# Four expert blocks per round on TensorE, their transpositions in one row, gathers two blocks and stores six blocks off the gate-up

## What is computed

```python
def step(out, ws):
    wg, wu, wd, we = ws
    inter = jax.nn.silu(x @ wg.T) * (x @ wu.T)
    return (out + inter @ wd.T * we[:, None], None)
out, _ = jax.lax.scan(step, jnp.zeros_like(x), (gate_proj, up_proj, down_proj, w_full.T))
```

## Time and profile before

| | us |
|---|---|
| median of 3 runs | 1127.13 |
| lowest and highest run | 1126.86, 1133.95 |
| profiled execution, its own time | 1126.25 |
| span in its trace, first to last instruction | 1124.4 |
| expert stage, first gate-up to the last scaled row | 646.1 to 1078.2 |
| sum-up and output after it | 1078.2 to 1124.4 |

### The profile page before, as it was taken

How to read it: one execution, slowest core, us unless ns; L and a number is a source line. 1 busy time by engine, 2 the same in 40 slices (tenths; PEclk the granted TensorE clock), 3 DMA queues, 4 the chain that set the end, 5 groups by cost and what they waited for, 6 DMA issues and landing times. The chain is left out here.

```text
span 1124.4 us, 25144 instructions
## 1 busy us (share of the span) xinstructions
PE 1069.0 (95%) x7622; PEld 658.7 (59%) x7622; DVE 700.2 (62%) x2440; ACT 656.4 (58%) x1339; POOL 451.1 (40%) x521
## 2 busy tenths in 40 slices
PE   6889999999999999999889699999999999999997
PEld 3465666666666656664666445555555555555576
DVE  6866566665656666662459765656556666565648
ACT  4325454545555444547445668777877777787730
POOL 4333132222122000000220157777777777777620
PEclk9999999999999999999999899999999999999999
DMA  7501030113111311102113386583748546667278
GB/s 246 116 11 33 18 67 3 40 24 54 32 33 32 49 28 23 24 2 58 39 44 98 99 185 212 186 251 116 228 134 262 177 144 200 185 216 265 92 298 291
DMA packets 81789, 129.66 MB, mean 115 GB/s; under 512 B 32884, under 2 KB 53109, under 8 KB 81142
## 3 DMA queue, kind: packets, MB, share of 16 engines
q1 hardware_dynamic: 61852, 77.13, 24.7%
q0 software_dynamic: 15360, 47.21, 13.1%
q10 hardware_dynamic: 4448, 3.72, 1.1%
HBM read 97.57 MB, written 30.05 MB: 113 GB/s over the span
## 5 line engine op out<-in xcount | busy, mean ns | idle before, releaser
L710 DVE CUSTOM_DVE_ANT_0 a_masked<-a_ps_s,a_mask 128x512 bf16<-128x512 f32 (+3 forms) x512 | 230.3, 487 | 159.8 <-PE a_ps_s L877 157.6
L623 ACT ACTIVATE a_probs<-a_ps_e 128x512 f32<-128x512 f32 (+1 forms) x384 | 188.1, 527 | 119.7 <-PE a_ps_e L898 118.4
L1924 PE MATMUL e_ps_gu<-e_w_gu,e_xT 128*64 x640 | 208.7, 469 | 2.4 <-ACT e_s_gu L1737 1.6
L1924 PE MATMUL e_ps_gu<-e_s_gu,e_xT 128*64 128x352 f32 x640 | 208.6, 469 | 0.0
L188 POOL DMA_INDIRECT yn<-rows,inv x160 | 159.3, 995 | 118.9 <-DVE inv L1456 59.7
L1698 POOL DMA_INDIRECT y<-e_y,dst x160 | 163.8, 1024 | 59.0 <-issue 29.2
L1949 PE MATMUL e_ps_y<-e_w_d,e_hT 88*64 x640 | 151.5, 379 | 0.9 <-DVE e_hT L1814 0.9
L1949 PE MATMUL e_ps_y<-e_s_d,e_hT 88*64 88x256 f32 x640 | 151.5, 379 | 0.0
L895 PE MATMUL a_ps_e<-a_qT,a_kT 75*128 75x512 bf16 (+3 forms) x512 | 140.9, 303 | 2.1 <-ACT a_probs L623 1.6
L877 PE MATMUL a_ps_s<-a_kT,a_qT 72*128 72x512 bf16 (+3 forms) x512 | 131.4, 299 | 4.7 <-DVE a_headmax L710 2.8
L1924 PEld LDWEIGHTS e_ps_gu<-e_w_gu,e_xT 128*64 128x64 f32 x640 | 81.7, 137 | 92.0 <-issue 89.3
(11 more groups left out here) (259 smaller groups left out, 1873.5 us busy)
## 6 DMA issues: line engine op xcount, KB each, us to landing
e_w_gu<-e_gu SPq DMA_DIRECT2D x64, 352.0 KB
e_w_d<-e_down SPq DMA_DIRECT2D x64, 176.0 KB
a_qT<-qk_parts SPq DMA_DIRECT2D x45, 192.0 KB
e_w_gu<-y SPq DMA_DIRECT2D x8, 768.0 KB
qk_parts<-a_stage SPq DMA_DIRECT2D x16, 256.0 KB, 2.6
qkv<-y SPq DMA_DIRECT2D x12, 256.0 KB
e_w_d<-y SPq DMA_DIRECT2D x4, 768.0 KB
yn<-rows,inv POOLq DMA_INDIRECT x160, 3.3
```

The lines of the kernel that those rows point to most:

```text
L623: nc.scalar.activation(probs[:, i % HKV, UCOL[u]:UCOL[u + 1]], ps_e[:, (i * 3 + u) % 2, 0:w], ACT.Exp, scale=SCALE0).then_inc(exp_done, 1)
L710: ins = V.tensor_tensor_reduce(masked[:, n % 2, c:c + w], ps_s[:, n % 2, c:c + w], mask[:, T - w:T], 1.0, -3e38, ALU.add, ALU.max, headmax ...
L1924: ins = nc.tensor.matmul(ps_gu[r * SEG:(r + 1) * SEG, j % 2, 0:2 * INTER1], xT[:, j // 2 % 2, j % 2, k * P + r * SEG:k * P + (r + 1) * SEG ...
```

## The change

PE, ACT and DVE now go through groups of four blocks. On PE a group is: gate-up of two blocks, down of two blocks of the group before, gate-up of two, down of two, then all sixteen transpositions: `h` of the group's first two blocks, the rows of the next four blocks, `h` of the last two. Gate-up writes three PSUM banks in turn (the third is `ps_yT`), the turned rows two (`ps_o` is the second). Silu writes straight into `h`, which has four slots, and `gate` works in place. On DVE the copies follow the order of the row. POOL gathers `i + 8` and stores `i - 6` in step `i`.

```diff
-        LEAD, BEHIND, NF = 2, 4, ring.FIRST
+        LEAD, BEHIND, NF = 0, 6, ring.FIRST
...
+        gu_bank = (ps_gu[:, 0, :], ps_gu[:, 1, :], ps_yT[:, :])
+        xT_bank = (ps_xT[:, :], ps_o[:, :])
...
-                if j >= 2:
-                    act.wait_ge(h_ready, j - 1)
-                nc.scalar.activation(sg[:, j % 2, :], ps_gu[:, j % 2, 0:INTER1], ACT.Silu)\
+                if j >= 4:
+                    act.wait_ge(hT_ready, j - 3)
+                nc.scalar.activation(h[:, j % 4, :], gu_bank[j % 3][:, 0:INTER1], ACT.Silu)\
...
+            for g in range(FOURS):
+                j = 4 * g
+                for k in range(3):
+                    gate(j + k)
+                    attention(*part(j + k))
+                    if j == 0 and k == 1:
+                        copy_x(1)
+                        weigh(2)
+                        weigh(3)
+                gate(j + 3)
+                copy_h(2 * g)
+                if g + 1 < FOURS:
+                    copy_x(2 * g + 2)
+                    copy_x(2 * g + 3)
+                copy_h(2 * g + 1)
+                attention(*part(j + 3))
+                if g + 1 < FOURS:
+                    for k in range(4, 8):
+                        weigh(j + k)
...
-                if j >= 2 and j % 2 == 0:
-                    pe.wait_ge(xT_copied, j // 2)
+                if j >= 4 and j % 2 == 0:
+                    pe.wait_ge(xT_copied, j // 2 - 1)
...
                 pe.wait_ge(w_copied, gate_up_copied(j))
+                if j >= 3:
+                    pe.wait_ge(h_ready, j - 2)
...
-            oldest, now = None, [expert_of(j) for j in range(2)]
+            oldest, now = None, [expert_of(j) for j in range(4)]
+            for g in range(FOURS + 1):
                 after = None
+                b, a = 4 * g, 4 * g - 4
+                for k in (0, 2):
+                    if g < FOURS:
+                        gate_up(b + k, now[k])
+                        gate_up(b + k + 1, now[k + 1])
+                        if b + k == 0:
+                            turn_pair(1)
+                    if g:
+                        down(a + k, oldest[k])
+                        down(a + k + 1, oldest[k + 1])
+                if g + 1 < FOURS:
+                    after = [expert_of(b + 4 + k) for k in range(4)]
+                if g < FOURS:
+                    turn_h(2 * g)
+                    if g + 1 < FOURS:
+                        turn_pair(2 * g + 2)
+                        turn_pair(2 * g + 3)
+                    turn_h(2 * g + 1)
                 oldest, now = now, after
```

More of the change, by code:

```diff
@@ L1530, in layer1_experts @@
         NS, NW, NY, NQ = ring.NS, ring.NW, SCATTERS, 8
-        PAIRED = NBLK // 2
-        LEAD, BEHIND, NF = 2, 4, ring.FIRST
+        PAIRED, FOURS = NBLK // 2, NBLK // 4
+        LEAD, BEHIND, NF = 0, 6, ring.FIRST
         FIRST_ROWS_AT = 100
@@ L1539, in layer1_experts @@
         weight = sbuf(ctx, nc, "e_weight", [P, NQ])
-        sg = sbuf(ctx, nc, "e_sg", [P, 2, INTER1])
-        h = sbuf(ctx, nc, "e_h", [P, 2, INTER1])
+        h = sbuf(ctx, nc, "e_h", [P, 4, INTER1])
         hT = sbuf(ctx, nc, "e_hT", [HI1, 2, 2, 2 * P])
@@ L1613, in add_up @@
             E.tensor_tensor(x_sb[:, i, :], x_sb[:, i, :], y8[f][:, 0:D], ALU.add).then_inc(done, 1)
[L1615 to L1620, removed]
+        gu_bank = (ps_gu[:, 0, :], ps_gu[:, 1, :], ps_yT[:, :])
+        xT_bank = (ps_xT[:, :], ps_o[:, :])
         def gate_up_copied(j):
-            return j + 1 if j < 2 else 4 * (j // 2) - 2 + j % 2 + 1
+            g, k = divmod(j, 4)
+            if j < 4:
+                return j + 1
+            return 8 * g + k - 1 if k >= 2 else 8 * g + k - 3
         def down_copied(j):
-            return 4 * (j // 2) + j % 2 + (5 if j + 2 < NBLK else 3)
+            g, k = divmod(j, 4)
+            last_four = 0 if g < FOURS - 1 else 2 if k < 2 else 4
+            return 8 * g + (7 if k < 2 else 9) + k - last_four
         def part(j):
@@ L1748, in _, with silu_exp @@
                 copy_gate_up(j, experts[j])
[L1749 to L1760, removed]
+            def silu_exp(j):
+                silu(j)
+                n, l, k = part(j)
+                if k == 5:
+                    act.wait_ge(s_ready, n * B + B)
+                    nc.scalar.activation(e1[:, :, :], s1[:, :, :], ACT.Exp,
+                                         scale=SCALE1).then_inc(e_ready, 1)
+            for g in range(FOURS + 1):
+                b, a = 4 * g, 4 * g - 4
+                if g < FOURS:
+                    experts += [expert_of(b + 2), expert_of(b + 3)]
+                    for j in (b, b + 1):
+                        silu_exp(j)
+                        copy_gate_up(j + 2, experts[j + 2])
+                if g:
+                    for j in (a, a + 1):
+                        copy_y(j)
+                        copy_down(j + 2, experts[j + 2])
+                if g < FOURS:
+                    if g < FOURS - 1:
+                        experts += [expert_of(b + 4), expert_of(b + 5)]
+                    for j in (b + 2, b + 3):
+                        silu_exp(j)
                         if j + 2 < NBLK:
                             copy_gate_up(j + 2, experts[j + 2])
[L1763 to L1768, removed]
+                for k in range(2):
+                    if g:
+                        copy_y(a + 2 + k)
+                    if g < FOURS:
+                        copy_down(b + k, experts[b + k])
             for i in range(NT):
@@ L1788, in copy_x @@
                 dve.wait_ge(xT_ready, 2 * m + 2)
-                V.tensor_copy(xT[:, m % 2].rearrange("p a c -> p (a c)"), ps_xT[:, :]).then_inc(xT_copied, 1)
+                V.tensor_copy(xT[:, m % 2].rearrange("p a c -> p (a c)"), xT_bank[m % 2]).then_inc(xT_copied, 1)
             def weigh(j):
@@ L1802, in gate @@
                 dve.wait_ge(silu_ready, j + 1)
-                if j >= 2:
-                    dve.wait_ge(hT_ready, j - 1)
-                V.tensor_tensor(h[:, j % 2, :], sg[:, j % 2, :], ps_gu[:, j % 2, INTER1:2 * INTER1],
+                V.tensor_tensor(h[:, j % 4, :], h[:, j % 4, :], gu_bank[j % 3][:, INTER1:2 * INTER1],
                                 ALU.mult).then_inc(h_ready, 1)
@@ L1924, in gate_up @@
                         ins = nc.tensor.matmul(
-                            ps_gu[r * SEG:(r + 1) * SEG, j % 2, 0:2 * INTER1],
+                            gu_bank[j % 3][r * SEG:(r + 1) * SEG, 0:2 * INTER1],
                             xT[:, j // 2 % 2, j % 2, k * P + r * SEG:k * P + (r + 1) * SEG],
@@ L1937, in transpose_h @@
                     ins = nc.tensor.transpose(ps_hT[0:HI1, c:c + P],
-                                              h[:, j % 2, k * HI1:(k + 1) * HI1], ident[:, :])
+                                              h[:, j % 4, k * HI1:(k + 1) * HI1], ident[:, :])
                 ins.then_inc(hT_ready, 1)
@@ L1958, in turn_pair, with turn_h @@
                     transpose_x(j)
+            def turn_h(m):
+                for j in (2 * m, 2 * m + 1):
+                    transpose_h(j)
             turn_pair(0)
-            oldest, now = None, [expert_of(j) for j in range(2)]
-            for m in range(PAIRED + 1):
+            oldest, now = None, [expert_of(j) for j in range(4)]
+            for g in range(FOURS + 1):
                 after = None
[L1964 to L1979, removed]
+                b, a = 4 * g, 4 * g - 4
+                for k in (0, 2):
+                    if g < FOURS:
+                        gate_up(b + k, now[k])
+                        gate_up(b + k + 1, now[k + 1])
+                        if b + k == 0:
+                            turn_pair(1)
+                    if g:
+                        down(a + k, oldest[k])
+                        down(a + k + 1, oldest[k + 1])
+                if g + 1 < FOURS:
+                    after = [expert_of(b + 4 + k) for k in range(4)]
+                if g < FOURS:
+                    turn_h(2 * g)
[3 more added lines that the diff above has]
+                    turn_h(2 * g + 1)
                 oldest, now = now, after
```

2 lines of the change are left out of this document (1 added, 1 removed).

## The result

The changed kernel takes 1153.57 us (median of 4 runs, 1152.59 to 1161.72) against 1126.99 for the kernel before in the same session (median of 4): ratio 1.0225, 95% interval 1.0196 to 1.0253. I had forecast slower, 1142, with a range of 1122 to 1152. The direction was right, the size too small.

What follows compares the result with a forecast made beforehand. PE was taken to bound the kernel, at 10.97 us per group against 10.54: 1126.25 - 1.0 (start) + 15.9 (37 groups x 0.43) + 1.6 (end) = 1142.75, stated as 1142 us, range 1122 to 1152.

Steps and rivals of the forecast that it cites:

- PE sets the pace: Expert stage: PE is busy for all 50 us of a window, 5.27 per pair, with POOL close behind at 5.14.
- fewer changes of tiling are worth 0.28 per group: PE's row of transpositions: tiling changes twice per four blocks instead of twice per pair, saving 0.28 us per group.
- The price is 0.31 per group: In the row: gate-up waits for DVE's copy of rows behind a copy of h; row 2.21 us instead of 1.90.
- PE runs dry for 0.35 to 0.6 us; I take 0.40: Ahead of the row: four register loads plus hand-over take 2.75 to 3.0 us against a sequencer lead of 2.4.
- the high end: Upper bound for the loads' cost per group: 0.65 us, four loads at the pace of the slower pair.
- I take no difference: At the four exponentials ACT is held by table loads before and after; PE's changed wait was costed at nothing.
- the cover of the loads: PE's sequencer running 2.4 us ahead of the array, taken as the same lead after the change, hiding that much loading.
- Start: Up to the gate-up of block 8: near 669.2 instead of 670.19, so -1.0 us; block 2's gate-up unchanged at 652.98.
- End: From the gate-up of block 156 to the last scaled row: 14.1 us instead of 12.5, so +1.6.
- 1 and 2: Rivals: loads and copies both hide, 1117 us (chance 0.08); only the loads hide, 1128 us (chance 0.22).
- Rival 3: In the row and ahead of it: copies hide, loads don't, 0.12 us more per group, 1131 us; chance 0.08.
- Rival 4: DVE comes late to the row behind an attention part; a fourth of the groups lose 1 us, 1151 us; chance 0.10.

Runs made afterwards that it cites:

- e7: e4 with the first two gates of a group put together on DVE, ahead of both attention parts; 1125.00 us, ratio 0.9950 to the kernel before.
- e1: Changed kernel with the four register loads split, two behind each pair of downs; 1134.78 us, ratio 1.0038 to the kernel before.
- e4: Changed kernel with loads split, rows turned first (two gate-up banks) and the exponential moved three blocks later; 1125.05 us, ratio 0.9950 to the kernel before.
- e6: Kernel before with only the register loads moved: four in a row in every second pair, none in the others; 1150.84 us, ratio 1.0151.
- e8: Changed kernel with each of the four register loads done twice, eight in a row; 1300.55 us in one run.
- e2: Changed kernel with rows of the next pair turned before h, and two gate-up banks instead of three; 1146.73 us, ratio 1.0137 to the kernel before.

## Why the prediction was right and wrong

**PE sets the pace, fewer changes of tiling are worth 0.28 per group.** Right for PE: 10.54 to 10.24 in ordinary groups once both waits were away. But POOL, read from two DMAs as 5.14 per pair, takes 5.24 on average (e7), which leaves 0.03 per pair and not 0.13.

**"The price is 0.31 per group" (copies on the path).** Right: with the loads split, e1 took 10.54 and e4 10.24, a difference of 0.30; the row of e1 lasts the 2.20 that the copies allow, that of e4 1.90.

**"PE runs dry for 0.35 to 0.6 us; I take 0.40" (loads).** Mechanism right, shown by e1, e6 and e8 from three sides; the size was off: 0.47 in the gap and 0.52 in the group. I had taken a low value within my bounds although a slower pair of loads was among the rows. The four span 2.7 to 3.4 us with the hand-over of 0.17 behind them (2.88 on average), and single groups lost up to 0.96, beyond the high end. 33 groups by about 0.1 make the 3.0 us.

**"I take no difference" (exponentials).** This step failed most: 1.78 more per group where the sum had 0.43. I compared ACT with ACT, before and after, and stopped at PE's wait. The failed step is the cover of the loads: their price was taken as if the lead were 2.4 everywhere. It is 2.4 only where the sequencer was not held just before; behind a late copy it was 1.25. An exponential adds 2.53 to an ordinary group (13.59 - 11.06), and added 1.27 in the kernel before. Of the 1.26 more, 1.16 is the gap ahead of the row (1.945 against 0.785), which is the loads without their lead; only 0.10 is left for the waits on ACT, so that part of "no difference" nearly held. e1 agrees: it took 1.42 off these groups, and the two loads still at the place left a gap of 0.61 in place of 0.31.

**Start.** Right within 0.2. The 2.4 us ahead of it lie in code that the change left alone, at two places of this execution. Early in layer 0 the clock stood at its half level: PE was 0.5 us ahead of the kernel before at 42 us and 1.3 behind it at 52. Both windows of 42 to 48 us, before and then after:

```profile
42.00:48.00 6.00, 4.53 (x22) 2.41 (x20) 4.56 (x16) 2.29 (x5) 4.42 (x6) 1.00 0.38 79
```

```profile
42.00:48.00 6.00, 5.19 (x14) 2.94 (x13) 4.50 (x15) 2.04 (x4) 4.55 (x6) 0.50 0.44 102
```

The other 1.2 us come at 153 us, where PE, at full clock, waits for a DMA:

```profile
153.93 0.39 PE L877 MATMUL a_ps_s<-a_kT,a_qT 72*128 72x512 bf16 x1 [1.04 <-DMA a_qT<-qk_parts]
```

**End.** 0.5 more than forecast: the last two downs wait for copied weights, 0.76 from the down before instead of 0.22, which the sum did not have.

```profile
1103.81 0.43 PE L1966 MATMUL e_ps_y<-e_w_d,e_hT 88*64 x1 [0.37 <-ACT e_s_d L1742]
```

**Rivals.** 1 and 2 needed a longer lead; it never exceeded 2.41. The depth of 64 that the Trainium skill gives ("TensorE: Matmul & The Clock Gate", "Architectural detail: the array is 16× 32×32, not 1× 128×128") did not show as more lead in any run here; what that count covers, the runs do not tell. Rival 3 fell with the row of 2.24. Rival 4 did not decide: in all 37 rows the first copy starts 0.64 or 0.65 after the row's start. A late DVE came in only where a bank was taken away (e2, e4). POOL idled, as foreseen, though its longest waits ended with DVE's row weights and not with gate-up (view of waits, after):

```profile
POOL yn L188 <- DVE e_pick L1808: 34.5, 29, 3.5
POOL yn L188 <- PE e_ps_gu L1941: 8.0, 10, 1.5
```

## What to carry to other kernels

A scalar load on PE's sequencer was free only up to what the sequencer was ahead; so split such loads, and read the lead from the trace at every kind of round, since a wait just before spends it. When an engine is late, follow its wait one step further: what stands behind the held instruction and had lived on the lead. And an edit that saves 0.3 per round can be real and still lose, when it puts two covered costs onto the path; its parts (loads, copies, order on ACT) could be taken apart without giving up the saving, until the next engine, here POOL, was the bound. Take the pace of that next engine from its mean over the stage: two neighbouring rows gave 10.28 per group, the mean 10.5.

## What the runs showed of the hardware

- The lead of TensorE's sequencer was the same to 0.01 us (2.40 to 2.41) in 32 of 33 ordinary groups, with 18 matmuls not yet started in each, and 1.25 with 10 in all four behind the late weights.
- A register load with its two register steps costs 0.66 us of the sequencer's time, measured by adding four (e8); the load itself is 0.30.
- Stalls of 0.3 to 1.8 us ahead of the row left the granted clock at 1.00 for the whole stage; behind 21 of the 33 ordinary gaps of 3.2 to 3.9 us (e8) it fell to half for a few us (0.64 to 0.67 in windows of 5 us), behind 12 it did not; the stage's mean was 0.89.
- Early in layer 0 PE stood idle for some 2.6 us in both profiled executions (38.4 to 41.1, and 38.1 to 40.7); one then ran at 1.00, the other at 0.50. The same instructions so came out 1.7 us apart.
- An indirect DMA of 128 rows took POOL 0.97 to 0.99 us in most cases, but some took up to 2.2 us (e7, 747.8 us); the means over the stage were 1.00 for gathers and 1.02 for stores.
